# Second sweep of a two-layer adaLN block: where the ten mixture chunks stand among twelve slots

## What is computed

```
h = layernorm(x) * (1 + ca) + sa
qf = exp(q @ proj - diag - max)                 # attention features of the queries
num, den = qf @ kv, qf @ sum(kf);  attn = num / den
out1 = layernorm(h + attn @ Wo)
x = x + ga * layernorm(out1 + elu(out1 @ W1 + b1) @ W2 + b2)
h = layernorm(x) * (1 + cb) + sb
shared = (silu(h @ sfc1) * (h @ sfc2)) @ sfc3
moe = sum over experts of dispatch * (silu(h @ w1[e]) @ w2[e])
out = x + gb * (moe + shared)
```

## Time and profile before

| | us |
|---|---|
| median of 3 runs | 3349.52 (3348.2 to 3349.67) |
| the profiled execution | 3352.36 |
| its span | 3350.5 |
| granted TensorE clock, mean | 0.935 |
| PE busy in the span | 2799.0 (84%) |
| ACT busy in the span | 2362.0 (70%) |
| DVE busy in the span | 2627.5 (78%) |

### The profile page before, as it was taken

How to read it: one execution, slowest core, us unless ns; L and a number is a source line. 1 busy time by engine, 2 the same in 40 slices (tenths; PEclk the granted TensorE clock), 3 DMA queues, 4 the chain that set the end, 5 groups by cost and what they waited for, 6 DMA issues and landing times. The chain is left out here.

```text
span 3350.5 us, 53343 instructions
## 1 busy us (share of the span) xinstructions
PE 2799.0 (84%) x15818; PEld 2100.6 (63%) x15818; DVE 2627.5 (78%) x4494; ACT 2362.0 (70%) x5178; POOL 911.7 (27%) x607
## 2 busy tenths in 40 slices
PE   2377898898898888888889898689999889999986
PEld 1054665665565565566566575577887777778775
DVE  2999999999999999999999952566666666666663
ACT  3456686686777767668667654468888888888873
POOL 0443333333333333333333310011111111111111
PEclk6588999999998999999999999899999999999998
DMA  2000000000000000000000001000000000000000
GB/s 111 8 4 13 20 4 20 17 3 20 17 10 14 17 20 3 20 17 3 20 17 0 18 18 60 32 15 18 28 17 17 21 21 17 17 17 28 17 9 15
DMA packets 49779, 64.40 MB, mean 19 GB/s; under 512 B 3585, under 2 KB 36417, under 8 KB 49185
## 3 DMA queue, kind: packets, MB, share of 16 engines
q1 hardware_dynamic: 47392, 54.93, 5.0%
q10 hardware_dynamic: 2304, 8.46, 0.6%
HBM read 41.78 MB, written 21.60 MB: 19 GB/s over the span
## 5 line engine op out<-in xcount | busy, mean ns | idle before, releaser
L792 POOL TENSOR_TENSOR acc<-acc,shared 128x1024 f32<-128x1024 f32 x256 | 607.3, 2372 | 1009.5 <-DVE shared L1107 952.7
L1107 DVE TENSOR_TENSOR_SCAN shared<-shared 128x1024 f32<-128x1024 f32 x256 | 585.2, 2286 | 13.2 <-issue 4.9
L921 PEld LDWEIGHTS bank<-one_sb,hid 128*128 128x128 f32 x4096 | 483.5, 194 | 31.0 <-issue 17.2
L921 PE MATMUL bank<-one_sb,hid 128*128 128x128 f32 x4096 | 485.3, 277 | 14.6 <-ACT hid L657 14.6
L869 PE MATMUL bank<-S,pick_sb 96*128 96x512 bf16 x512 | 209.7, 414 | 249.3 <-DVE shared L1119 136.6
L625 ACT ACTIVATE shared<-shared,aneg 128x512 f32<-128x512 f32 (+1 forms) x512 | 341.3, 722 | 63.3 <-DVE shared L1107 47.7
L158 POOL TENSOR_SCALAR n_ve<-n_mv 128x4 f32<-128x4 f32 x96 | 57.8, 602 | 1163.1 <-DVE n_mv L141 1163.1
L869 PEld LDWEIGHTS bank<-S,pick_sb 96*128 96x128 bf16 x512 | 50.1, 98 | 442.5 <-DVE shared L1119 199.8
L1119 DVE TENSOR_TENSOR shared<-shared,bank 128x1024 f32<-128x1024 f32 x256 | 312.5, 1221 | 12.1 <-PE bank L869 1.9
L1100 DVE TENSOR_TENSOR shared<-shared,bank 128x1024 f32<-128x1024 f32 x256 | 309.6, 1209 | 0.4 <-PE bank L869 0.3
L657 ACT ACTIVATE hid<-banks,one_sb 128x512 f32<-128x512 f32 x304 | 208.2, 691 | 109.1 <-PE bank L921 65.4
(11 more groups left out here) (274 smaller groups left out, 7008.3 us busy)
## 6 DMA issues: line engine op xcount, KB each, us to landing
kv_dram<-Gs ACTq DMA_DIRECT2D x16, 516.5 KB, 3.1
kvl<-kv_dram SPq DMA_DIRECT2D x16, 516.5 KB, 3.5
xs<-in_x SPq DMA_DIRECT2D x16, 256.0 KB, 2.9
x<-in_x SPq DMA_DIRECT2D x16, 256.0 KB, 3.0
x_dram<-x SPq DMA_DIRECT2D x16, 256.0 KB, 2.1
h_dram<-hT SPq DMA_DIRECT2D x16, 256.0 KB, 2.0
h<-h_dram SPq DMA_DIRECT2D x16, 256.0 KB, 2.6
x2s<-x_dram SPq DMA_DIRECT2D x16, 256.0 KB, 2.6
```

Source lines behind the costliest of these rows:

```text
L792: pool.tensor_tensor(acc[:, :, :], acc[:, :, :], zz[:, k % 2, :, :], ALU.add)\
L921: last = pe.matmul(bank1(f"down{e}")[:, j * D:(j + 1) * D], hid[:, e % 2, f, j * P:(j + 1) * P], w2[:, e, f, :], start=(f == 0), stop=(f = ...
L1107: dve.tensor_tensor_scan(h[:, :, :].rearrange("p g t -> p (g t)"), dec[:, k % 2, :, :].rearrange("p g t -> p (g t)"), u[:, :, :].rearrange ...
```

## The change

Chunks 1 and 2 leave slots 2 and 3. Slots 2 and 3 now hold no chunk; slots 4 to 7 hold chunks 1 to 4; slots 8 and 9 hold two chunks each (5, 6 and 7, 8), the second of them in a new table `XR`, run after the slot's turns; chunk 9 stays in slot 10 and chunk 0 in slot 1. `DOWN` is shifted to match. In slots 4 and 6 ACT runs the `qT` and `aT` copies and the exponential before silu, so that two silus stand next to each other. The second chunk of slots 8 and 9 comes on DVE after `quotient`.

```diff
-        XQ = {q + 1: q for q in range(NX)}
-        DOWN = {6: (0,), 7: (1, 2), 8: (3,), 9: (4, 5), 10: (6,), 11: (7,)}
+        XQ = {1: 0, 4: 1, 5: 2, 6: 3, 7: 4, 8: 5, 9: 7, 10: 9}
+        XR = {8: 6, 9: 8}
+        EXP_FIRST = (4, 6)
+        DOWN = {6: (0,), 7: (1,), 8: (2, 3), 9: (4,), 10: (5, 6), 11: (7,)}
...
-                        if e is not None and slot in XQ:
+                        if e is not None and slot in XQ and slot not in EXP_FIRST:
                             silu(XQ[slot], e)
-                        if c is not None and slot < M:
+                        if c is not None and slot < M and slot not in EXP_FIRST:
                             feature(slot, c)
...
                             keep_quotient(at_slot(slot, 3), c)
+                        if c is not None and slot in EXP_FIRST:
+                            feature(slot, c)
+                        if e is not None and slot in EXP_FIRST:
+                            silu(XQ[slot], e)
+                        if e is not None and slot in XR:
+                            silu(XR[slot], e)
...
+                        if e is not None and slot in XR:
+                            hidden(XR[slot], e, s)
+                            factor(XR[slot], e, s)
...
                             quotient(at_slot(slot, 2), c)
+                        if e is not None and slot in XR:
+                            chunk(XR[slot], e)
```

More of the change, by code:

```diff
@@ L1432, in sweep_two @@
                 q = XQ[slot]
+                orderD += [(f"x{q}", MOE, sl_ok, q + 1), (f"y{q}", MOE, hm_ok, q + 1)]
+            if slot in XR:
+                q = XR[slot]
                 orderD += [(f"x{q}", MOE, sl_ok, q + 1), (f"y{q}", MOE, hm_ok, q + 1)]
```

## The result

| | before | after |
|---|---|---|
| median, us | 3349.6 | 3502.9 (3499.5 to 3504.9, 4 runs) |
| ratio, 95% interval | | 1.0457 (1.0444 to 1.0470) |
| profiled execution, us | 3352.4 | 3504.9 |
| one step of the second sweep, us | 73.85 | 85.35 |

The direction was right. The size was not: +153 us against a forecast of +125, and 2.9 us over the top of the range.

A forecast was written before the change was run, and what follows sets the result against it. PE was taken as the fuller engine (busy 66.85 of 73.90 us a step). Slots +8.1 us a step over 14 steps, +113, clock +18, ends -6: +125 us, 3474.5 us; range 3445 to 3500.

The forecast's parts named there:

- What goes from ACT: ACT, each step: 8 table loads of 1.283 us go, 10.3 us, worth something only where ACT's own queue ends last.
- Slots 2 and 3: Chunks 1 and 2 leave: square of slot 2 to slot 4 takes 15.50 us instead of 15.82, 0.3 us less.
- Slot 4: Late silu delays DVE's chunk, hE and PE's product; +4.2 us a step, slots 2 and 3's 0.3 already off.
- Slots 7 to 10: Late silu of slot 6 and doubled chunks: +0.7, +2.4, +0.6 and +0.2 us a step for slots 7, 8, 9, 10.
- The ends: Step 16, without attention, gets shorter as ACT's loads and silus count there: -6 us (0 to -9); step 17: 0.
- The clock: PE's clock drops behind slot 4's new hole, 1.4 us nine times in ten: 1.25 us a step, +18 us.
- the low clock spreads: Rival: slots 2, 3 and 7 get more holes too, two clock drops a step: 3495 us; chance 0.09.

The follow-up runs named there:

- the order alone: Kernel before with only ACT's order of slots 4 and 6 changed (copies and exponential ahead of silu), chunks in their old places: 3457.3 us, ratio 1.0322.
- the kernel with slot 4 filled: Changed kernel with four more runs of slot 4's numerators on PE in its hole, the wait for hE kept: 3465.9 us, ratio 1.0352.
- elu ahead of the chunk: Changed kernel with DVE's elu tiles of slots 3 and 4 moved ahead of the slot's chunk: 3411.0 us, ratio 1.0185.
- The places alone: Changed kernel with silu back in front of the exponential in slots 4 and 6, chunks as in the change: 3389.7 us, ratio 1.0124.
- the kernel with slot 2 filled: Changed kernel with slot 2's d product run three times and its numerators twice on PE, filling only that slot's holes: 3489.7 us, ratio 1.0415.

## Why the prediction missed, step by step

- **What goes from ACT: right.** 10 us of ACT time a step and no gain on the path. The rule of the Trainium skill on grouping activations by table ("ScalarE: Activation LUTs", "Table sets: the hidden batching unit") speaks for the other sign; the order alone, with half of the loads saved, was 108 us slower.
- **Slots 2 and 3: right in kind.** Step 1 foretold 15.50 us; the kernel with slot 4 filled takes 15.49 us in its step 6, at full clock (square at 2568.39, slot 4 at 2583.88). In the change it was 16.18, 0.68 more, by the clock.
- **Slot 4: right**, 10.12 us against 10.14, and shown by two runs: the order alone makes the hole, elu ahead of the chunk removes it.
- **Slots 7 to 10: right**, 27.9 us against 27.6; the difference is slot 7's. The places alone confirm them: 3389.7 us, in the range of 3384 to 3394 that was worked out, after the result, from nearly the same terms.
- **The ends: right in the number**, -6 us: from step 16's line 1604 to the end of the span 78.5 us, 84.6 before. In part this is luck: 1.45 us of it is step 16's product, which ran at the low clock before (3.26 us, rows 9) and takes 1.81 us now, behind 1.45 us of idle time; the forecast had no such term.
- **The clock: the term that failed.** It had 1.25 us a step and measured 3.35. Two things in it were mis-sized. A drop was priced from rows 9 by the product alone, 1.4 us, and its tail into slot 5 (1.05 us) left out; here it costs 1.62 + 1.05 = 2.67. And a second drop in slot 2 was held unlikely, since slot 2 of step 1 has such holes at full clock; it came in 13 of 14 steps, 0.68 us. The rival "the low clock spreads", given 9 in 100, is what happened, at 47 us instead of 39. 14 x (3.35 - 1.25) = 29 us is about the whole miss of 28; the small differences of the other terms nearly cancel.

The trace of before had rows against that last argument, in the same step 1 that was called as the witness: a drop behind short holes, where slot 6 ends and slot 7 begins.

```profile
2205.02 0.66 PE L1782 MATMUL bank<-keep_sb,at 128*128 128x128 f32 x4 [1.35 <-DVE uq L1950]
2206.17 0.50 PE L174 MATMUL bank<-high,h3l 128*128 128x512 f32 x1 [0.49 <-ACT qT L1584]
...
2206.96 1.89 PE L1790 MATMUL bank<-shared,aT 128*128 128x128 f32 x8
```

Eight records that take 1.05 us one slot earlier (at 2200.59) take 1.89 here, and the granted clock from 2206.9 to 2209.9 is 0.51.

On the frequency of slot 4's drop the forecast was right: it came in every step. The Trainium skill's section "HAM oscillation — how this bites in real kernels" ("TensorE: Matmul & The Clock Gate") says that a wait in every pass brings a cold start in every pass; the trace agrees, at 4.4 us of wait. It would have changed the forecast by 2 us only, since the frequency of that drop was not what failed.

## What to carry to other kernels

Before an operation is moved back on one engine, follow its reader on the next engine and list what is queued behind that reader: here a silu moved back behind two copies, the second of which waits for TensorE, and an exponential held two unrelated elu tiles and, through them, TensorE for 4.4 us. Saved table loads are worth nothing where the engine waits anyway, and a step of the same trace without the work in question tells in one subtraction what removing it is worth. When a change opens a hole of some microseconds on TensorE in every pass, price the matmuls behind it at half clock until the profile shows them fast, the next stage's too. One pass at full clock behind a hole does not clear the other passes: count the passes that have the drop.

## What the runs showed of the hardware that was not expected

Adding 3.6 us of matmuls to a wait made each step 3.35 us shorter (85.35 to 82.0). And the same holes do not bring the same clock: behind the same hole of 1.5 us, in the same slot of the same kernel, the granted clock is 1.00 in 12 steps and falls in 2 (down to 0.52 in step 11). A drop also stood behind holes of only 1.35 and 0.49 us (step 1 of the kernel before), and the drop behind a hole of 4.4 us cost 1.4, 2.3 and 2.8 us in three steps running, in the kernel with slot 2 filled.
